# Layer 2's key, value and query products in a two-layer graph attention kernel: four-pass float32 against three float16 products

## The chip, the cores and the metric

The kernel runs on one core of a Trainium2 chip. The metric is the device time of one launch in microseconds (us). TensorE (PE) multiplies matrices, VectorE (DVE), ScalarE (ACT) and GpSimd (POOL) work element by element, SyncE (SP) issues nearly all DMAs.

## The reference

N = 3125 nodes with 128 features, and 103125 directed edges, self loops among them. Two TransformerConv layers run over the same edges, the first with 4 heads of 128 channels (512 features out, then relu), the second with 2 heads that are averaged. The result is added to x and each row is normalized.

```python
def transformer_conv(x, src, dst, Wq, bq, Wk, bk, Wv, bv, Ws, bs, H, C, concat):
    q = (x @ Wq + bq).reshape(n, H, C)      # k and v alike
    alpha = jnp.einsum('ehc,ehc->eh', q[dst], k[src]) / jnp.sqrt(jnp.float32(C))
    p = jnp.exp(alpha - amax[dst])          # softmax over the edges of a destination
    out = jax.ops.segment_sum(p[:, :, None] * v[src], dst, num_segments=n)
    out = out / denom[:, :, None]
    out = out.reshape(n, H * C) if concat else out.mean(axis=1)
    return out + x @ Ws + bs
h = jax.nn.relu(transformer_conv(x, ..., H1, C1, True))
out = transformer_conv(h, ..., H2, C2, False)
x = _layernorm(x + out, axis=-1)
```

## The kernel before

The graph is turned into a dense mask: a 3125 x 3125 table of the logarithm of how often each edge occurs, built in 87 batches (`mask_and_projections`) and kept in DRAM (`mask_scratch`). DVE compares edge ends with index rows ("hot" tiles), PE sums them, ACT takes the logarithm, SP stores it. Layer 1's K and V are computed between the batches. Attention is then dense: for each of 25 tiles of 125 destinations and each head there is one slot, numbered s, in which every engine does its share for slots s to s+3.

A slot of `attention` on PE has seven steps k. It holds the scores of 3125 sources in seven pieces, each three float16 products of a high and a low part (`scores`), 9 transposes of probabilities, 25 blocks of values (two float16 matmuls each, `product`), and at k=3 the query of slot s+3 (`query`). DVE adds the mask and takes the maximum (`masked_scores`), ACT does exponentials and high parts (`exponentials`, `part_hi`), POOL the low parts and the end of each row (`low_parts`, `finish`, `query_parts`), and SP's DMA transposes (`flip`) turn the first 16 blocks of probabilities. In layer 1's head 0, PE turns the finished rows of the tile before (`rows_transposed`, k=4) into PSUM bank `B_skip`, ACT applies the relu out of it, and PE then writes the tile's skip product into the same bank (`skip_product`, k=6), for which it waits for the relu (semaphore `s_r`). SP stores the relu's rows to `hT_scratch`.

Between the layers the hidden features hT (128 x 4 x 3125 float32, feature chunks k = 0 to 3 of 128) are loaded from `hT_scratch` into the tile `room`. `projections2` computes layer 2's K in 7 pieces of 512 nodes for 2 heads, and V in 25 blocks, each as four float32 matmuls accumulated in PSUM; ACT, POOL and DVE split the results. A float32 matmul is two records in the trace, and so x8 is one head's piece of K and x8 one block of V. Layer 2's queries are four float32 matmuls of 125 columns per slot, over 50 slots. `W` is the room of layer 2's weights, in the tile `spare`; POOL multiplies them in tiles 2 to 4 of layer 1 (`weights_scaled`).

The order of work on each engine is written out by hand in these functions, with semaphores between engines. Each block (mask, layer 1, projections, layer 2) ends when all engines have reached its end, SP with its last DMA issue too.

## Time and profile before

| | |
|---|---|
| median of 3 runs | 1863.93 us (1863.75 to 1864.02) |
| the profiled execution: time, span | 1863.01 us, 1861.2 us |
| PE, DVE, ACT, POOL busy | 95%, 81%, 67%, 61% |
| mean granted TensorE clock | 0.985 |
| mask and layer 1's K and V | 0 to about 220 us |
| layer 1's attention | about 225 to 1224 us |
| layer 2's K and V | 1226.8 to 1316 us |
| layer 2's attention | 1317.7 us to the end |

Busy time of PE is counted from the start to the modelled end of each matmul, and neighbours overlap, so a busy share near 100% says only that PE seldom stands idle. What a matmul costs in a dense stretch is the distance between the starts of neighbours.

### The profile page before, as it was taken

To read this page: it belongs to the slowest core of one execution; us is meant where nothing else is said; L and a number is where in the kernel's file an instruction comes from. 1 tells how busy PE (TensorE), PEld (TensorE's weight loads), DVE (VectorE), ACT (ScalarE), POOL (GpSimd) and SP (SyncE) were. 2 spreads that over 40 slices of the span, in tenths; PEclk is the share of its full clock that TensorE was granted. 3 is DMA by queue.
4 is the path that set the end of the run, shared out by engine and by line. 5 is a ranking of instruction groups with operands and counts; after the bars stand their busy time and mean duration, and the time that the engine had idled before them with its cause. 6 is when DMAs were issued, how large, how long until landed. Compare 5 with 4: busy or idle time off the path is not lost. (4 is left out here: it accounts for less than half of the span.)

```text
span 1861.2 us, 44238 instructions
## 1 busy us (share of the span) xinstructions
PE 1768.3 (95%) x14644; PEld 1328.6 (71%) x14644; DVE 1507.8 (81%) x4506; ACT 1255.4 (67%) x2090; POOL 1137.0 (61%) x1432
## 2 busy tenths in 40 slices
PE   3789799999999999999999999989899999999997
PEld 2556467777777777777777777756677787777876
DVE  7999889888888888888888788724688888988886
ACT  4579877777777677777777777721466667766675
POOL 4200067777776777777677776723477676766765
PEclk9899899999999999999999999999999999999999
DMA  6879868777888888888778887690488898888885
GB/s 164 221 210 264 233 116 151 156 148 151 159 157 156 154 150 157 159 154 154 152 156 153 159 159 151 117 255 4 88 173 169 182 174 179 174 179 180 181 176 109
DMA packets 753649, 301.72 MB, mean 162 GB/s; under 512 B 655853, under 2 KB 734065, under 8 KB 750171
## 3 DMA queue, kind: packets, MB, share of 16 engines
q1 hardware_dynamic: 752252, 296.96, 78.4%
q8 instruction: 122, 2.00, 0.5%
q0 software_dynamic: 640, 1.63, 0.3%
q14 instruction: 107, 0.87, 0.2%
q10 hardware_dynamic: 528, 0.26, 0.1%
HBM read 93.62 MB, written 47.83 MB: 76 GB/s over the span
## 5 line engine op out<-in xcount | busy, mean ns | idle before, releaser
L1383 POOL TENSOR_TENSOR prob_parts_l<-prob_l,prob_parts_l 125x512 f16<-125x512 f32 x600 | 721.2, 1233 | 13.5 <-ACT prob_parts_l L1470 13.5
L1461 ACT ACTIVATE prob_l<-prob_l,neg_max_l 125x1024 f32<-125x1024 f32 (+1 forms) x450 | 521.6, 1161 | 5.3 <-DVE neg_max_l L1553 5.3
L1729 PE MATMUL score_l<-room,QT_l 128*128 128x512 f16 (+2 forms) x2100 | 512.4, 353 | 1.4 <-DVE scale_rows L1701 1.2
L1476 ACT CAST probT_l<-transposed_l 128x375 f16<-128x375 f32 x450 | 213.5, 475 | 427.3 <-PE transposed_l L1753 427.3
L1768 PE MATMUL output_l<-V,prob_flipped_l 128*128 128x256 f16 x2400 | 459.6, 272 | 4.2 <-DMA prob_flipped_l<-prob_parts_l 4.1
L1770 PE MATMUL output_l<-V,prob_flipped_l 128*128 128x128 f16 x2400 | 427.5, 219 | 0.0
L1545 DVE CUSTOM_DVE_ANT_0 prob_l<-score_l,mask_even 125x512 f32<-125x512 f32 (+2 forms) x546 | 333.9, 615 | 113.7 <-PE score_l L1729 112.1
L1545 DVE CUSTOM_DVE_ANT_0 prob_l<-score_l,mask_odd 125x512 f32<-125x512 f32 (+2 forms) x504 | 308.9, 615 | 108.1 <-PE score_l L1729 106.9
L1470 ACT CAST prob_parts_l<-prob_l 125x1024 f16<-125x1024 f32 x300 | 309.5, 1033 | 0.1
L1768 PEld LDWEIGHTS output_l<-V,prob_flipped_l 128*128 128x128 f16 x2400 | 233.6, 97 | 56.5 <-issue 6.4
L1768 PE MATMUL output_l<-V,probT_l 128*128 128x256 f16 x1350 | 271.2, 273 | 2.8 <-DVE probT_l L1558 1.6
L1558 DVE TENSOR_TENSOR probT_l<-transposed_l,probT_l 128x375 f16<-128x375 f32 x450 | 244.9, 544 | 22.1 <-ACT probT_l L1476 14.0
L1729 PE MATMUL score_l<-KT,QT_l 128*128 128x512 f16 (+2 forms) x1050 | 255.1, 353 | 2.2 <-DVE piece_max_l L1545 2.2
L1770 PEld LDWEIGHTS output_l<-V,prob_flipped_l 128*128 128x128 f16 x2400 | 234.2, 98 | 28.5
L1729 PEld LDWEIGHTS score_l<-room,QT_l 128*128 128x128 f16 x2100 | 187.5, 98 | 91.5 <-issue 12.7
L1770 PE MATMUL output_l<-V,probT_l 128*128 128x128 f16 x1350 | 246.5, 219 | 0.0
L1371 POOL CAST QT_l<-q_now_l 128x125 f16<-128x125 f32 x150 | 43.8, 292 | 329.4 <-ACT q_now_l L1444 329.4
L1753 PE MATMUL transposed_l<-ident,prob_l 125*128 125x125 f32 (+1 forms) x1350 | 218.9, 270 | 5.9 <-ACT prob_l L1461 5.2
L1753 PEld LDWEIGHTS transposed_l<-ident,prob_l 125*128 125x128 f32 (+1 forms) x1350 | 171.7, 139 | 55.0 <-ACT prob_l L1461 3.8
L1768 PEld LDWEIGHTS output_l<-V,probT_l 128*128 128x128 f16 x1350 | 131.0, 97 | 67.3 <-DVE probT_l L1558 19.4
L1770 PEld LDWEIGHTS output_l<-V,probT_l 128*128 128x128 f16 x1350 | 131.8, 98 | 29.0
L1531 DVE SCALAR_TENSOR_TENSOR mask_even<-mask_even 125x512 f32<-125x512 f32 (+2 forms) x168 | 135.8, 808 | 0.0
(201 smaller groups left out, 2354.1 us busy)
## 6 DMA issues: line engine op xcount, KB each, us to landing
mask_scratch<-log SPq DMA_DIRECT2D x87, 420.0 KB
mask_even<-mask_scratch SPq DMA_DIRECT2D x25, 448.0 KB
mask_odd<-mask_scratch SPq DMA_DIRECT2D x24, 448.0 KB
mask_odd<-mask_scratch SPq DMA_DIRECT2D x12, 896.0 KB
mask_even<-mask_scratch SPq DMA_DIRECT2D x12, 896.0 KB
prob_flipped_l<-prob_parts_l SPq DMA_TRANSPOSE x600, 3.2
hT_scratch<-rowsT_l SPq DMA_DIRECT2D x24, 250.0 KB, 3.6
mask_odd<-mask_scratch SPq DMA_DIRECT2D x12, 471.2 KB
```

The source lines that it names most:

```text
L1371: pool.tensor_copy(QT[:, u, 0, 0:TP], q_now[:, u, :]).then_inc(s_qh, 1)
L1383: pool.tensor_tensor(parts[0:TP, 1, a:b], prob[:, h % 2, a:b], parts[0:TP, 0, a:b], ALU.subtract).then_inc(s_flo, 1)
L1461: act.activation(e, e, ACT.Exp, bias=neg_max[:, h % 2:h % 2 + 1], accum_out=total[:, h % 2, c:c + 1]).then_inc(s_exp, 1)
L1470: act.copy(parts[0:TP, 0, a:b], prob[:, h % 2, a:b]).then_inc(s_fhi, 1)
L1476: act.copy(probT[:, q, 0, 0:n, 0:TP], flipped_in_psum(h, q, n)).then_inc(s_hi, 1)
L1531: dve.scalar_tensor_tensor(piece, piece, STEEP, piece, ALU.mult, ALU.min).then_inc(s_cleared, 1)
L1545: dve.tensor_tensor_reduce(out=prob[:, h % 2, a:b], in0=score_bank(h, p)[0:TP, 0:b - a], in1=mask[parity][:, a:b], scale=1.0, scalar=-3.0e ...
L1558: dve.tensor_tensor(probT[:, q, 1, 0:n, 0:TP], flipped_in_psum(h, q, n), probT[:, q, 0, 0:n, 0:TP], ALU.subtract).then_inc(s_t, 1)
L1729: last = pe.matmul(score_bank(h, p)[:, 0:b - a], QT[:, h % 2, i, :], KT[:, h, j, a:b], start=n == 0, stop=n == len(products) - 1)
L1753: last = pe.transpose(flip_bank(h, q)[0:w, i * TP:(i + 1) * TP], prob[:, h % 2, b * C:b * C + w], ident[0:TP, 0:TP])
L1768: pe.matmul(O[:, 0:2 * C], hi, V[:, b, h, :, :].rearrange("p a c -> p (a c)"), start=start, stop=False, skip_group_check=True)
L1770: return pe.matmul(O[:, 0:C], lo, V[:, b, h, 0, :], start=False, stop=stop, skip_group_check=True)
```

## The change

Layer 2's K, V and queries become three float16 products each (high by high, high by low, low by high), twelve matmuls where there were four. For this hT and the weights are split into a float16 high and low part. The two parts of a feature lie next to each other, in the tile that is stored, in DRAM and in `room`, so that hT keeps its bytes and one part is read at a step of two float16. Before the split each hidden feature is brought into a fixed range: a power of two per feature is worked out from a bound (`h_row`, `h_up`) and multiplied into layer 1's skip weights, skip bias and `v_back`, and taken back out of layer 2's weights (`h_back`). The relu is now ACT's high part, and a new DVE instruction takes the low part (`rows_low`); `s_r`, for which PE's skip product and SP's store wait, is given by DVE. ACT's relu moves ahead of the third exponential. Layer 2's skip product stays float32: POOL joins the two parts of a tile's features first (`features`, into `h_now`). The weights are split in tiles 10 to 13 of layer 1, and lie first in `xT`'s room, since they are split in place.

```diff
+H_UP = 2.0 ** 3
+SPLIT_TILE = 10
+PRODUCTS = ((0, 0), (0, 1), (1, 0))
...
-    hT_dram = nc.dram_tensor("hT_scratch", (C, H1, N), F32, kind="Internal").ap()
+    hT_dram = nc.dram_tensor("hT_scratch", (C, H1, 2 * N), F16, kind="Internal").ap()
...
         room = sb("room", [C, H1 * N])
         spare = sb("spare", [C, 3 * H1 * H2 * C])
-        hT = room[:, :].rearrange("c (k n) -> c k n", k=H1)
+        hT = room[:, :].bitcast(F16).rearrange("c (k n a) -> c a k n", a=2, k=H1)
...
+                        dve.scalar_tensor_tensor(h_row, bank[7][:, :], TINY, abs_bs, ALU.max, ALU.add).then_inc(s_h_row, 1)
...
+                        dve.tensor_tensor(h_row, h_row, abs_rows[:, 2, :], ALU.add).then_inc(s_h_row, 1)
+                    if b == HIDDEN_AT + 1:
+
+                        dve.wait_ge(s_h_row, 2)
+                        dve.tensor_scalar(h_row.bitcast(I32), h_row.bitcast(I32), EXPONENT, None, ALU.bitwise_and).then_inc(s_h_row, 1)
+                        dve.wait_ge(s_h_row, 3)
+                        dve.tensor_scalar(h_up.bitcast(I32), h_row.bitcast(I32), -1, INVERSE_UP, ALU.mult, ALU.add).then_inc(s_h_row, 1)
...
+                        dve.tensor_scalar(second["h_back"][:, :], bank[LIST_BANK][:, 0:H1], 1.0 / H_UP, None, ALU.mult)
...
+                pool.wait_ge(s_h_row, 4)
+                for to, up in ((L["v_back"][:, :], h_up), (L["Ws"][:, 0, :], h_up), (L["bs"], h_up[0:TP, :])):
+                    pool.tensor_tensor(to, to, up, ALU.mult).then_inc(s_h_scaled, 1)
...
+                pool.wait_ge(s_late, 16)
+                pool.tensor_tensor(L["Ws"][:, :, :], L["Ws"][:, :, :], second["h_back"][:, :].unsqueeze(2).broadcast_to([C, H1, C]),
+                                   ALU.mult).then_inc(s_back, 1)
...
                         for k in range(H1):
-                            last = pe.matmul(bank[n % 2][:, 0:b - a], Wk_sb[:, k, h * C:(h + 1) * C],
-                                             hT[:, k, a:b], start=k == 0, stop=k == H1 - 1)
+                            for m, (i, j) in enumerate(PRODUCTS):
+                                last = pe.matmul(bank[n % 2][:, 0:b - a], Wk_sb[:, k, i, h * C:(h + 1) * C], hT[:, j, k, a:b],
+                                                 start=k == m == 0, stop=k == H1 - 1 and m == len(PRODUCTS) - 1)
...
                         for k in range(H1):
-                            last = pe.matmul(bank[2 + t % 2][0:r, 0:H2 * C], hT[:, k, t * C:t * C + r], Wv_sb[:, k, :],
-                                             start=k == 0, stop=k == H1 - 1)
+                            for m, (i, j) in enumerate(PRODUCTS):
+                                last = pe.matmul(bank[2 + t % 2][0:r, 0:H2 * C], hT[:, i, k, t * C:t * C + r], Wv_sb[:, k, j, :],
+                                                 start=k == m == 0, stop=k == H1 - 1 and m == len(PRODUCTS) - 1)
...
-                    sp.dma_start(hT_dram[:, :, bass.ds(t * TP, TP)], rowsT[:, :].rearrange("c (h n) -> c h n", h=H)
+                    sp.dma_start(hT_dram[:, :, bass.ds(2 * t * TP, 2 * TP)], rowsT_pairs[:, :, :].rearrange("c (h n) a -> c h (n a)", h=H)
...
+                def weights_back(n, i):
+
+                    w = second["W"][i]
+                    pool.wait_ge(s_scaled2, 2 * n + 1)
+                    pool.tensor_tensor(w, w, second["h_back"][:, :].unsqueeze(2).broadcast_to([C, H1, H2 * C]), ALU.mult
+                                       ).then_inc(s_scaled2, 1)
+
+                def features(t):
+
+                    wait(pool, s_sp, t)
+                    hi, lo = (featT[:, a, :, t * TP:(t + 1) * TP] for a in range(2))
+                    pool.tensor_tensor(h_now[:, :, :], hi, lo, ALU.add).then_inc(s_h_now, 1)
...
+                        if layer == 1 and h == 2 and 2 <= t <= 4:
+                            weights_back(t - 2, (0, 2, 1)[t - 2])
+                        if layer == 2 and h == 1 and exists(t + 1):
+                            features(t + 1)
...
-                        act.activation(rowsT[:, :], B_skip[:, 0:H * TP], ACT.Relu).then_inc(s_r, 1)
+                        act.activation(rowsT[:, 0, :], B_skip[:, 0:H * TP], ACT.Relu).then_inc(s_rhi, 1)
+
+                def weights_hi(n):
+
+                    act.wait_ge(s_scaled2, 6)
+                    if n == 0:
+                        act.wait_ge(s_sp, -(-H1 * H2 * C // TP))
+                    else:
+                        act.wait_ge(s_wlo, n)
+                    act.copy(w16_at[n][:, :, 0, :], second["W"][n]).then_inc(s_whi, 1)
...
-                            exponentials(s + 1, hn, 2)
                         if layer == 1 and h == 0 and not is_first(t):
                             rows_transposed(t - 1)
+                        if exists(tn):
+                            exponentials(s + 1, hn, 2)
+                        if layer == 1 and h == 2 and 0 <= t - SPLIT_TILE < 3:
+                            weights_hi(t - SPLIT_TILE)
...
+                def rows_low(t):
+
+                    dve.wait_ge(s_rhi, t + 1)
+                    if t == NT - 1:
+                        hi, lo = (hT[:, a, :, H_LATE:N] for a in range(2))
+                        dve.scalar_tensor_tensor(lo, B_skip[:, 0:H * TP].rearrange("c (k n) -> c k n", k=H), 0.0, hi,
+                                                 ALU.max, ALU.subtract).then_inc(s_r, 1)
+                    else:
+                        dve.scalar_tensor_tensor(rowsT[:, 1, :], B_skip[:, 0:H * TP], 0.0, rowsT[:, 0, :],
+                                                 ALU.max, ALU.subtract).then_inc(s_r, 1)
+
+                def weights_low(n):
+
+                    if n < 3:
+                        dve.wait_ge(s_whi, n + 1)
+                        dve.tensor_tensor(w16_at[n][:, :, 1, :], second["W"][n], w16_at[n][:, :, 0, :], ALU.subtract).then_inc(s_wlo, 1)
+                    else:
+                        dve.wait_ge(s_wlo, 3)
+                        dve.tensor_copy(second["W16"][0], first_w16).then_inc(s_w16, 1)
...
+                            if layer == 1 and h == 0 and k == 5 and not is_first(t):
+                                rows_low(t - 1)
+                            if layer == 1 and h == 3 and k == 3 and 0 <= t - SPLIT_TILE < 4:
+                                weights_low(t - SPLIT_TILE)
...
+                if layer == 1:
+                    rows_low(NT - 1)
...
-                    for k in range(KC):
-                        last = pe.matmul(B_q[:, 0:TP], Wq[:, k, h * C:(h + 1) * C], featT[:, k, bass.ds(t * TP, TP)],
-                                         start=k == 0, stop=k == KC - 1)
+                    if layer == 1:
+                        last = pe.matmul(B_q[:, 0:TP], Wq[:, 0, h * C:(h + 1) * C], featT[:, 0, t * TP:(t + 1) * TP],
+                                         start=True, stop=True)
+                    else:
+                        for k in range(KC):
+                            for m, (i, j) in enumerate(PRODUCTS):
+                                last = pe.matmul(B_q[:, 0:TP], Wq[:, k, i, h * C:(h + 1) * C], featT[:, j, k, t * TP:(t + 1) * TP],
+                                                 start=k == m == 0, stop=k == KC - 1 and m == len(PRODUCTS) - 1)
                     last.then_inc(s_qp, 1)
...
-                        last = pe.matmul(B_skip[0:TP, 0:W], featT[:, k, t * TP:(t + 1) * TP], Ws[:, k, :], start=k == 0, stop=k == KC - 1)
+                        pe.wait_ge(s_h_now, t + 1)
+                        for k in range(KC):
+                            last = pe.matmul(B_skip[0:TP, 0:W], h_now[:, k, :], Ws[:, k, :], start=k == 0, stop=k == KC - 1)
                     last.then_inc(s_sp, 1)
```

**Hand-over in layer 1.** The next rows are ACT's at the end of tile 1's head 0 in layer 1 (`prob_l` are probabilities, `prob_parts_l` their high parts, `rowsT_l` the relu's rows), before:

```order
L1444 ACTIVATE q_now_l<-query_l,bq_scaled_l 128x125
L1470 CAST prob_parts_l<-prob_l 125x1024
L1461 ACTIVATE prob_l,total_l<-prob_l,neg_max_l 125x1077
L1455 ACTIVATE rowsT_l<-skip_rows_l 128x500
L1476 CAST probT_l<-transposed_l 128x3x125 x3
```

and now:

```order
L1538 CAST prob_parts_l<-prob_l 125x1024
L1503 ACTIVATE q_now_l<-query_l,bq_scaled_l 128x125
L1538 CAST prob_parts_l<-prob_l 125x1024
L1514 ACTIVATE rowsT_l<-skip_rows_l 128x500
L1529 ACTIVATE prob_l,total_l<-prob_l,neg_max_l 125x1077
L1544 CAST probT_l<-transposed_l 128x3x125 x3
```

The relu changes places with the third exponential (125x1077). At the same place DVE has, at steps k=5 and 6 of head 0 (`ISA` rows are the masked scores and the reading of their maximum), before:

```order
L1576 TENSOR_SCALAR weight_l<-neg_max_l,inv_l 125x1
L1609 TENSOR_SCALAR scale_rows<-scale_rows 128x256
L1545 ISA prob_l,piece_max_l<-score_l,mask_odd 125x512
L1545 ISA piece_max_l 125x1
L1531 SCALAR_TENSOR_TENSOR mask_even<-mask_even 125x512
L1611 TENSOR_SCALAR scale_rows<-scale_rows 128x256
L1545 ISA prob_l,piece_max_l<-score_l,mask_odd 125x384
```

and now:

```order
L1680 TENSOR_SCALAR scale_rows<-scale_rows 128x256
L1616 ISA prob_l,piece_max_l<-score_l,mask_odd 125x512
L1616 ISA piece_max_l 125x1
L1705 SCALAR_TENSOR_TENSOR rowsT_l<-skip_rows_l,rowsT_l 128x500
L1602 SCALAR_TENSOR_TENSOR mask_even<-mask_even 125x512
L1682 TENSOR_SCALAR scale_rows<-scale_rows 128x256
L1616 ISA prob_l,piece_max_l<-score_l,mask_odd 125x384
```

The subtraction that makes the low part stands between the masked scores and the clearing of the next mask piece (`mask_even`). This recurs in each tile from 1 to 24.

**Layer 2's projections and queries on PE.** From the start of `projections2` (`room` is hT, `spare` the weights), before:

```order
L1168 MATMUL proj_bank<-room,spare 128x512 x4
L1158 MATMUL proj_bank<-ident,scale_rows 128x1 x4
L1168 MATMUL proj_bank<-room,spare 128x512 x4
L1178 MATMUL proj_bank<-spare,room 128x256 x16
L1168 MATMUL proj_bank<-room,spare 128x512 x8
L1178 MATMUL proj_bank<-spare,room 128x256 x16
```

and now:

```order
L1196 MATMUL proj_bank<-room,spare 128x512 x12
L1185 MATMUL proj_bank<-ident,scale_rows 128x1 x4
L1196 MATMUL proj_bank<-room,spare 128x512 x12
L1207 MATMUL proj_bank<-spare,room 128x256 x48
L1196 MATMUL proj_bank<-room,spare 128x512 x24
L1207 MATMUL proj_bank<-spare,room 128x256 x48
```

Each group is three times as long, and nothing moves. The query is alike: `query_l<-room,spare 128x125 x4` becomes x12 in every slot.

**Features on POOL.** The end of one of layer 2's tiles on POOL, from the head-0 slot's low parts, before:

```order
L1401 TENSOR_TENSOR rows_l<-summed_l,skip_l 125x128
L1371 CAST QT_l<-q_now_l 128x125
L1373 TENSOR_TENSOR QT_l<-q_now_l,QT_l 128x125
L1383 TENSOR_TENSOR prob_parts_l<-prob_l,prob_parts_l 125x512 x4
L1391 TENSOR_TENSOR summed_l<-summed_l,v_back 125x128
L1394 TENSOR_SCALAR summed_l<-summed_l,weight_l 125x128
L1404 TENSOR_TENSOR xres<-summed_l,rows_l 125x128
L1371 CAST QT_l<-q_now_l 128x125
L1373 TENSOR_TENSOR QT_l<-q_now_l,QT_l 128x125
L1383 TENSOR_TENSOR prob_parts_l<-prob_l,prob_parts_l 125x512 x4
```

and now:

```order
L1441 TENSOR_TENSOR rows_l<-summed_l,skip_l 125x128
L1411 CAST QT_l<-q_now_l 128x125
L1413 TENSOR_TENSOR QT_l<-q_now_l,QT_l 128x125
L1423 TENSOR_TENSOR prob_parts_l<-prob_l,prob_parts_l 125x512 x4
L1464 TENSOR_TENSOR h_now_l<-room 128x500
L1431 TENSOR_TENSOR summed_l<-summed_l,v_back 125x128
L1434 TENSOR_SCALAR summed_l<-summed_l,weight_l 125x128
L1444 TENSOR_TENSOR xres<-summed_l,rows_l 125x128
L1411 CAST QT_l<-q_now_l 128x125
L1413 TENSOR_TENSOR QT_l<-q_now_l,QT_l 128x125
L1423 TENSOR_TENSOR prob_parts_l<-prob_l,prob_parts_l 125x512 x4
```

One join of two parts (`h_now_l`) follows the low parts of every second slot, ahead of the end of the row.

## Rows read from the trace of the kernel before

**Rows 1.** Busy time by stretch: span, then PE, PEld, DVE, ACT, POOL, clock, DMA, GB/s.

```profile
140.00:170.00 30.00, 28.54 (x247) 19.33 (x245) 30.00 (x18) 29.62 (x44) 0.00 (x0) 1.00 0.98 268
240.00:1190.00 950.00, 944.87 (x8053) 708.95 (x8054) 788.40 (x2622) 692.42 (x1185) 686.59 (x870) 1.00 0.81 153
...
1340.00:1780.00 440.00, 437.79 (x3843) 347.57 (x3842) 376.64 (x1263) 295.32 (x504) 310.25 (x377) 1.00 0.87 176
```

**Rows 2.** Who waited in 1340 to 1780 us: total, times, longest.

```profile
POOL QT_l L1371 <- ACT q_now_l L1444: 92.0, 41, 3.3
DVE prob_l L1545 <- PE score_l L1729: 55.9, 68, 1.9
...
PE score_l L1729 <- DVE piece_max_l L1545: 2.2, 2, 2.0
```

**Rows 3.** PE in layer 2's projections: start, length, instruction.

```profile
1236.38 7.07 PE L1178 MATMUL proj_bank<-spare,room 128*128 128x256 f32 x32
1243.28 7.03 PE L1168 MATMUL proj_bank<-room,spare 128*128 128x512 f32 x16
1250.15 7.07 PE L1178 MATMUL proj_bank<-spare,room 128*128 128x256 f32 x32
```

**Rows 4.** PE at a query of layer 2, and what follows it.

```profile
1599.32 1.11 PE L1717 MATMUL query_l<-room,spare 128*128 128x125 f32 x8
1600.27 0.81 PE L1729 MATMUL score_l<-KT,QT_l 128*128 128x512 f16 x3
```

**Rows 5.** PE, eight value matmuls of layer 1, each with its weight load.

```profile
564.05 0.27 PE L1768 MATMUL output_l<-V,prob_flipped_l 128*128 128x256 f16 x1
564.16 0.22 PE L1770 MATMUL output_l<-V,prob_flipped_l 128*128 128x128 f16 x1
...
564.71 0.65 PE L1729 MATMUL score_l<-room,QT_l 128*128 128x384 f16 x3
```

**Rows 6.** PE, a batch of the mask: twelve 160-column matmuls, each with a weight load.

```profile
151.71 0.99 PE L954 MATMUL mask_banks<-hot 128*128 128x160 bf16 x12 [0.19 <-DVE hot L782]
152.53 1.04 PE L917 MATMUL mask_banks<-xT,Wk_sb 128*128 128x500 f32 x2
```

**Rows 7.** Layer 1, head 0 of one tile: ACT, DVE and PE from step k=5.

```profile
564.23 1.20 ACT L1461 ACTIVATE prob_l<-prob_l,neg_max_l 125x1077 f32<-125x1077 f32 x1
...
565.05 0.97 DVE L1531 SCALAR_TENSOR_TENSOR mask_odd<-mask_odd 125x512 f32<-125x512 f32 x1
...
565.41 0.57 ACT L1455 ACTIVATE rowsT_l<-skip_rows_l 128x500 f32<-128x500 f32 x1
...
566.03 0.29 PEld L1739 LDWEIGHTS skip_rows_l<-Ws_sb,xT 128*125 128x125 f32 x2 [0.24 <-ACT rowsT_l L1455]
...
567.49 0.48 PE L1753 MATMUL transposed_l<-ident,prob_l 125*128 125x125 f32 x3
```

**Rows 8.** The tile skip_rows_l: DVE's add from PSUM, and the waits on the relu.

```profile
L1681 DVE TENSOR_TENSOR skip_l<-skip_rows_l,bias_room x25: 677/681/692, 252.9 to 1196.9; 125x512 f32<-125x512 f32 x25
...
  ACT rowsT_l L1455: 5.5, 23
```

**Rows 9.** Groups by line: a small DVE step of the mask, POOL's low parts.

```profile
L254 DVE TENSOR_SCALAR room<-v_back 128x512 int32<-128x512 int32 x1 | 0.4, 427 | 0.0
...
L1383 POOL TENSOR_TENSOR prob_parts_l<-prob_l,prob_parts_l 125x512 f16<-125x512 f32 x600 | 721.2, 1233 | 13.5 <-ACT prob_parts_l L1470 13.5
```

**Rows 10.** DVE in the mask stage, while POOL works and after it.

```profile
55.41 3.20 DVE L782 TENSOR_TENSOR hot<-row_iota,rel 128x2880 bf16<-128x2880 f16 x1
...
64.38 1.66 DVE L782 TENSOR_TENSOR hot<-row_iota,rel 128x2880 bf16<-128x2880 f16 x1
```

**Rows 11.** The end of layer 1: SP's issue of loads, the last relu, the first product.

```profile
1220.83 5.31 SPq L1360 DMA_DIRECT2D room<-hT_scratch  x2
...
1224.08 0.59 ACT L1452 ACTIVATE room<-skip_rows_l 128x500 f32<-128x500 f32 x1 [8.18 <-PE skip_rows_l L1745]
...
1226.84 5.08 PE L1168 MATMUL proj_bank<-room,spare 128*128 128x512 f32 x8 [2.79 <-PEq L1294]
```

More of the change, by code:

```diff
@@ L99 @@
 INVERSE = 254 << 23
+INVERSE_UP = (254 + 3) << 23
 EPS_DENOM = 1e-16
@@ L333, in mask_and_projections @@
         bv_sb, abs_ws = (k_room[:, 2 * N + i * H1 * C:2 * N + (i + 1) * H1 * C] for i in range(2))
-        abs_bs, h_row = (k_room[0:1, 2 * N + i * H1 * C:2 * N + (i + 1) * H1 * C] for i in range(2, 4))
+        abs_bs, h_row = (k_room[:, 2 * N + i * H1 * C:2 * N + (i + 1) * H1 * C] for i in range(2, 4))
+        h_up = abs_bs
         minus = sb("minus_ident", [C, C], F16)
@@ L1430, in _ @@
                 low_parts(0, 0)
+                if layer == 2:
+                    features(0)
                 over_tiles(tile)
@@ L1726, in scores @@
                     wait(pe, s_masked, NP * s + p + 1 - score_bank_back(h, p))
[L1727 to L1728 removed]
+                    for n, (i, j) in enumerate(PRODUCTS):
                         last = pe.matmul(score_bank(h, p)[:, 0:b - a], QT[:, h % 2, i, :], KT[:, h, j, a:b],
[L1730 removed]
+                                         start=n == 0, stop=n == len(PRODUCTS) - 1)
                     last.then_inc(s_score, 1)
@@ L1735, in skip_product @@
                         wait(pe, s_r, t)
+                        last = pe.matmul(B_skip[0:TP, 0:W], featT[:, 0, t * TP:(t + 1) * TP], Ws[:, 0, :], start=True, stop=True)
                     else:
                         wait(pe, s_skip, t)
-                    for k in range(KC):
-                        last = pe.matmul(B_skip[0:TP, 0:W], featT[:, k, t * TP:(t + 1) * TP], Ws[:, k, :], start=k == 0, stop=k == KC - 1)
+                        pe.wait_ge(s_h_now, t + 1)
+                        for k in range(KC):
+                            last = pe.matmul(B_skip[0:TP, 0:W], h_now[:, k, :], Ws[:, k, :], start=k == 0, stop=k == KC - 1)
                     last.then_inc(s_sp, 1)
```

53 lines of the change are left out of this document (32 added, 21 removed).

## Prediction

> **What bounds the kernel now.** I read the busy time by stretch first [rows 1]. In layer 1 (240 to 1190 us) and layer 2 (1340 to 1780 us) PE is busy 99% of the time at a granted clock of 1.00, DVE 83% and 86%. Busy is not bound, so the waits come next [rows 2]: in 440 us of layer 2 PE waited 2.2 us for DVE's maxima, DVE 55.9 us for PE's scores and POOL 92.0 us for the query that PE starts. PE sets the pace there; a microsecond taken from its queue is a microsecond of the span, as long as DVE keeps its 55.9 us in hand. In the projections PE's groups follow each other without a gap: K's two heads of a piece (x16) start 6.87 us before the next group, four blocks of V (x32) 6.90 us [rows 3]. The mask stage is different: in 140 to 170 us DVE is busy for all of 30.00 us [rows 1], so what is added to DVE there lengthens the stage.
>
> **K and V.** A head's piece of K takes 6.87 / 2 = 3.44 us, a block of V 6.90 / 4 = 1.73 us. The price of a float16 product I take from eight value matmuls, four of 256 and four of 128 columns, each with its own weight load: 564.05 to 564.71, 0.66 us for 1536 columns [rows 5], 0.43 ns a column, 0.22 us for 512 columns, 0.11 us for 256. Twelve make 2.64 us and 1.32 us. K gives back 12 x 0.80 = 9.6 us, and the last piece of 53 columns some 0.5 us (estimated as 2 x 12 products at 0.055 us, the price of 128 columns, against the same four passes); V 25 x 0.41 = 10.2 us. Together 20.3 us. The split after them keeps up: DVE has per block of V two steps of 256 columns (some 0.35 us each, half of the 0.68 us for 512 [rows 8]) and a clearing of up to 0.97 us [rows 7], 1.6 us against 1.32 us on PE. In four blocks it falls 1.1 us behind, less than the one block that the second bank holds, and K's two heads (5.3 us) let it catch up. I charge 0.5 us for this and for the weight splits below.
>
> **Queries.** A query takes 1600.27 - 1599.32 = 0.95 us [rows 4]. Twelve products of 125 columns cost 12 x 0.43 x 125 = 0.65 us by the column, 12 x 0.055 = 0.66 us by the same rows. All 50 queries lie on PE's path: 14.5 us. Here nothing of before shows 125-column products one behind the other, each with a weight load. The nearest row is the mask's batch, twelve products of 160 columns in 152.53 - 151.71 = 0.82 us, 0.068 us each [rows 6], which is the columns' price again (160 x 0.43 = 0.069), so no floor shows at 0.068. Bounds: 0.82 us a query (saves 6.5 us), and 0.65 us (15 us). I take 0.66, since within the value matmuls a 128-column product with its load does fit into 0.055 us: the pair of 256 and 128 takes 0.165, of which the 256 columns need 0.11.
>
> The Trainium skill says otherwise ("TensorE: Matmul & The Clock Gate", Back-to-back issue gap): pairs of weight load and matmul are said to sustain about 81 ns per matmul at 128 columns. By it a query would be 0.97 us and the queries would give back nothing; the value matmuls and the mask's 0.068 us speak against it.
>
> **The step of two float16.** hT is read as moving operand (K, queries) and loaded as weights (V) at a step of two elements, 4 bytes. No row shows this. Rows at both ends: contiguous float16 moves 2 bytes per 0.43 ns. Float32 with its four passes moves 4 bytes per column and pass in two records, 0.43 us per record of 512 columns [rows 3], that is 4.8 bytes per ns, just as contiguous float16 has 4.7. If bytes spanned were the limit, a stepped product would cost 0.43 us per 512 columns, twice my price. I take the column's price, as columns per pass explain all rows too (512 columns in two passes at 2.4 GHz), and keep the other as a rival.
>
> The Trainium skill ("SBUF — State Buffer", Door 1: The DMA port swizzle) has accesses to one 16-byte line at full bandwidth if at least two hit it, a free step of up to 8 bf16; a step of two hits four times and would be free. No run yet shows it.
>
> **Hand-over in layer 1.** PE's skip product waits for the relu 23 times, 5.5 us in all [rows 8], 0.24 us each. In the tile shown ACT starts the third exponential at 564.23 and the relu at 565.41, and PE goes on at 566.03 [rows 7]. Now the relu comes first and ends at about 564.23 + 0.57 = 564.80, and DVE, which is free at 565.05, subtracts: 0.68 us for 500 columns out of PSUM, from the add of the same bank [rows 8], to 565.73, before PE gets there at about 565.8. The wait goes: -4.5 us (bounds: -5.5, and +3 if DVE is 0.1 us later than the relu was). The exponential ends 0.57 us later, at about 566.1; its reader on PE starts at 567.49 [rows 7], so 1.4 us cover it. Behind the subtraction on DVE stand a clearing of the mask and the next masked scores, which have the slack that DVE has each slot. If that cover were gone, 24 x 0.68 = 16 us would stand there. SP's store of the rows waits for DVE instead of ACT and gets its rows earlier.
>
> **The mask stage.** DVE gets two small steps of 512 columns, 0.43 us each [rows 9], and one of 4 columns: +1.0 us. POOL gets three multiplications of 512 columns, about 1.2 us each [rows 9], 3.7 us. DVE's comparison of 2880 columns takes 3.20 us while POOL works and 1.66 us when it doesn't [rows 10]: 1.54 us lost in 3.20. By that 3.7 us of POOL cost DVE 1.5 us (0 to 1.8). Sum +2.5 us (1 to 3).
>
> **What is hidden.** POOL's join of features, 25 of about 1.2 us [rows 9], stands behind the low parts, and POOL waits 92.0 us in 42 slots for queries [rows 2], 2.2 us a slot. Without this cover it would be 30 us. The row's end is 1.2 us later and has its next reader a slot on. POOL's three multiplications of weights (1024 columns, some 2.5 us each by twice the price of 512) in layer 1 meet the same wait. ACT's three casts and DVE's four steps for the weights, about 1 us each, take ACT's and DVE's idle time, in four tiles; bounded by 4 us. At the end of layer 1 the low part of the last rows comes 0.7 us after the relu (1224.67), at 1225.4; SP issues loads until 1220.83 + 5.31 = 1226.14 and PE starts at 1226.84 [rows 11], so SP still ends the block. DMAs carry the same bytes in the same runs. The multiplication of Ws on POOL in `projections2` waits for a load; the first cast behind it may be 1 us late, while PE has one bank more to fill. PE's start at a lower clock (5.08 us for a piece of 3.44 [rows 11]) stays as it is.
>
> **Sum.** -20.3 - 14.5 - 4.5 + 2.5 + 0.5 = -36.3 us. The profiled execution took 1863.0 us, 0.9 us less than the median: 1826.7 us, and 1827.6 us against the median.
>
> **Rivals.**
> - The step costs (moving operand at half rate). K: 12 x (12 x 0.43 - 3.44) = +20.6 us; a query 12 x 0.43 x 125 x 2 = 1.29 us, +17 us; V and the rest as above: -10.2 - 4.5 + 3.0. Sum +26 us: 1890 us, slower. It decides from a price of about 1.5 columns per column on. For it: nothing excludes it; against it: passes explain the rows as well. 9%.
> - Products of 125 columns with a load have a floor at 0.068 us or above (0.08 us: the rule above). The queries give 6.5 us or nothing: 1836 to 1842 us. The rows speak against it. 10%.
> - Something in layer 1 takes the place of the removed wait: PE waits for DVE's subtraction, or DVE, pushed back 0.68 us, hands PE its maxima later. +0.2 us in each of 24 tiles instead of -0.2: 1837 us; that DVE is idle for 17% of layer 1 [rows 1] speaks against it. 9%.
> - Layer 2 does not stay with PE: after 0.29 us less a slot DVE's idle time of 1.3 us a slot shrinks to 1.0, and POOL is 1.2 us busier in every second slot. A third of the queries' gain lost, with some of the joins: 1835 us. 10%.
> - The forecast, all terms about as above: 62%, own range 1821 to 1834 us.
>
> **Numbers.** 1827.6 us. The forecast and its three rivals on the same side reach from 1821 to 1842 us; with the bounds of the small terms I give 1820 to 1846 us, which leaves the stepped case and some mishap out. A difference of 0.2%, 3.7 us, is about what a measurement of this kernel can tell from none. Faster 0.89, same 0.02, slower 0.09.
>
> **What would show it.** Right: K's group of a piece about 5.3 us instead of 6.87, V's of four blocks 5.3 instead of 6.90, a query 0.66 us from its start to the next instruction, no wait for `rowsT_l` before the skip product, layer 1's attention begun 2 to 3 us later, DVE's idle time in layer 2 lower and PE's waits still a few us. Wrong: matmuls of `room` whose starts lie 0.43 us apart for 512 columns (the step), 0.08 us for 125 (the load), PE waiting for `rowsT_l` of DVE or `piece_max_l` in layer 1, or for `h_now_l` in layer 2.

## Result and the profile after

| | before | after |
|---|---|---|
| median, 4 runs each | 1863.97 us (1863.75 to 1864.87) | 1842.86 us (1840.68 to 1843.64) |
| ratio, 95% interval | | 0.9884 (0.9867 to 0.9901) |
| profiled span | 1861.2 us | 1841.3 us |
| PE, DVE, ACT, POOL busy | 95%, 81%, 67%, 61% | 95%, 85%, 69%, 64% |

The changed kernel is 21 us faster, where 36 us were forecast: the direction and the range held, the size did not. Two places answer well to the rows of before. In layer 2's projections PE's groups are (start, length, instruction; they answer to [rows 3]):

```profile
1239.06 5.62 PE L1196 MATMUL proj_bank<-room,spare 128*128 128x512 f16 x24
1244.52 5.40 PE L1207 MATMUL proj_bank<-spare,room 128*128 128x256 f16 x48
1249.76 5.62 PE L1196 MATMUL proj_bank<-room,spare 128*128 128x512 f16 x24
```

K's group now starts 5.46 us before the next one, not 6.87, and V's 5.24 us, not 6.90. And a query of layer 2, with what follows it (answers to [rows 4]), takes 0.70 us, not 0.95:

```profile
1646.95 0.86 PE L1819 MATMUL query_l<-room,spare 128*128 128x125 f16 x12
1647.65 0.81 PE L1830 MATMUL score_l<-KT,QT_l 128*128 128x512 f16 x3
```

The places where the time went are found by PE's first query of each stage. These rows are the first query of layer 1, the first of layer 2, and one of head 0 in tile 16 and in tile 24 of layer 2, after:

```profile
228.91 0.54 PE L1814 MATMUL query_l<-xT,Wq_sb 128*128 128x125 f32 x1 [6.27 <-PEq L501]
...
1297.85 0.89 PE L1819 MATMUL query_l<-room,spare 128*128 128x125 f16 x7 [2.82 <-PEq L1083]
...
1626.31 0.86 PE L1819 MATMUL query_l<-room,spare 128*128 128x125 f16 x12
...
1791.56 0.62 PE L1819 MATMUL query_l<-room,spare 128*128 128x125 f16 x8
```

| place | before | after | moved by | forecast |
|---|---|---|---|---|
| first query of layer 1 | 225.07 | 228.91 | +3.8 | +2.5 |
| a query of layer 1's last tile | 1179.49 | 1178.18 | -5.2 | -4.5 |
| first query of layer 2 | 1317.72 | 1297.85 | -18.6 | -20.3 + 0.5 |
| end of the span | 1861.2 | 1841.3 | 0.0 | -14.5 |

("moved by" counts from the row above.) So what is missing is missing in layer 2's attention. Outside it, the mask stage lost 1.3 us more than forecast and the projections gave 1.2 us less, and the hand-over in layer 1 gave 0.7 us more. Each query of layer 2 is 0.25 us shorter, fifty of them, and the attention is as long as it was (543.5 us both; 541.2 us in e11, a second trace of the changed kernel). The waits of 440 us of it, 1320 to 1760 us (answers to [rows 2]):

```profile
POOL QT_l L1411 <- ACT q_now_l L1503: 77.7, 42, 5.6
DVE prob_l L1616 <- PE score_l L1830: 40.0, 48, 1.5
PEld output_l L1871 <- DVE probT_l L1629: 16.3, 40, 1.0
...
PE score_l L1830 <- DVE piece_max_l L1616: 3.0, 2, 2.7
```

DVE's wait for scores fell from 55.9 to 40.0 us. The third row is new among the first: PE's weight loads for the value matmuls wait 40 times for DVE's low part of `probT`, which stands in the queue just behind the query. PE got there earlier and DVE did not. The same wait in 440 us of before, and of the runs e2 and e1 below, whose queries are longer and shorter than the changed kernel's:

```profile
PEld output_l L1768 <- DVE probT_l L1558: 1.7, 6, 0.3
PEld output_l L1874 <- DVE probT_l L1629: 1.7, 5, 0.5
PEld output_l L1870 <- DVE probT_l L1629: 23.3, 47, 1.8
```

It grows as the query shrinks. A weight load runs ahead of the matmuls, so only a part of these waits holds up the products themselves.

A table of how long a tile (two heads) of layer 2 takes helps below. Each number is the distance of two first queries of tiles, divided by the tiles between them (eight or nine, tiles 15 or 16 to 24); after, (1791.56 - 1626.31) / 8.

| kernel | PE in a query | a tile |
|---|---|---|
| before | 0.95 us | 20.95 us |
| after | 0.70 us | 20.66 us |
| e1, 4 products | 0.23 us | 20.16 us |
| e2, 17 products | 0.99 us | 21.03 us |
| e3, features joined once | 0.70 us | 20.51 us |
| e7, skip product in float16 | 0.70 us | 20.31 us |

### The profile page after: what moved, and what is told of

The parts are those of the page before. It is cut to its first block and busy times, and to the rows that moved or that the text cites. A ratio compares the mean times of both kernels' runs of the same rounds, so it can differ in the third digit from the quotient of the medians.

```text
span 1841.3 us, 45045 instructions
## 1 busy us (share of the span) xinstructions
PE 1742.8 (95%) x15000; PEld 1301.7 (71%) x15000; DVE 1561.1 (85%) x4538; ACT 1262.7 (69%) x2093; POOL 1175.7 (64%) x1464
## 5 line engine op out<-in xcount | busy, mean ns | idle before, releaser
L1602 DVE SCALAR_TENSOR_TENSOR mask_even<-mask_even 125x512 f32<-125x512 f32 (+2 forms) x168 | 151.1, 899 | 0.0
```

The source lines that it names most:

```text
L1602: dve.scalar_tensor_tensor(piece, piece, STEEP, piece, ALU.mult, ALU.min).then_inc(s_cleared, 1)
```

## Experiments

Ratios are to the kernel before, timed beside each. The theories: (A) VectorE takes over the pace of layer 2's slots, (B) PE keeps it and the gain is lost elsewhere, (C) GpSimd's new work slows VectorE.

**How much a query's time is worth.** e1_short_query puts one product in place of three (it leaves out the crossed ones), e2_long_query puts five more in front of them, as here:

```diff
+                        for r in range(5):
+                            pe.matmul(B_q[:, 0:TP], Wq[:, r % KC, 0, h * C:(h + 1) * C], featT[:, 0, r % KC, t * TP:(t + 1) * TP],
+                                      start=True, stop=True)
```

> Layer 2's queries sum the high-by-high products alone: 4 products instead of 12, so a query is about 0.46 us shorter on TensorE (0.69 to 0.23 at 0.0575 us a product); the crossed products of the queries are left out. Theory A: in layer 2 VectorE's chain sets the slot, and what TensorE saves it spends waiting for VectorE's low part of probT; then 50 x 0.46 = 23 us off TensorE give little, 1837 to 1843. Theory B: TensorE sets the slot and the missing gain is lost elsewhere (the joined features on GpSimd, the clock at the layer's start); then nearly all comes through, about 1820.

> Layer 2's queries get five more products ahead of their sum (17 instead of 12), so a query takes about 0.69 + 5 x 0.0575 = 0.98 us, as long as it took in float32 (0.95). Theory A (VectorE sets the slot of layer 2): 50 x 0.29 = 14 us more on TensorE show as 0 to 5 us, 1843 to 1848. Theory B (TensorE sets it): about 1857.

e1: 1827.57 us, ratio 0.9803 (0.9789 to 0.9816), 14 to 15 us less than the changed kernel (against its second and first series, e11) for 23 us of PE. e2: 1850.29 us, 0.9924 (0.9911 to 0.9938), 7 to 9 us more for 14.5. Neither theory alone: in a tile e1 takes 0.92 us from PE and gets 0.50 us, e2 adds 0.59 us and pays 0.37. With the joins on GpSimd in place, about half to two thirds of PE's time reaches the slot, on both sides of the changed kernel. The tile of e2 is 0.08 us longer than that of the kernel before (21.03 against 20.95 us), which is what its two queries take more: behind a query of that length the joins cost nothing.

**The joined features.** e3_features_once leaves 24 of 25 additions out; each tile's skip product reads the first tile's features.

```diff
-                        if layer == 2 and h == 1 and exists(t + 1):
-                            features(t + 1)
...
-                        pe.wait_ge(s_h_now, t + 1)
+                        pe.wait_ge(s_h_now, 1)
```

> GpSimd joins the two parts of layer 2's features for the first tile only, and every tile's skip product reads that one; 24 additions of 1.035 us go from GpSimd, and the skip rows of tiles 1 to 24 are those of tile 0. Theory C: these additions slow VectorE beside them (mask clears and low parts); 25 us of such overlap at the ratio of row 10 would give 5 to 10 us back, 1833 to 1838. Theory A or B without it: 1841 to 1844.

1837.33 us, 0.9857 (0.9842 to 0.9873): 4 to 5.5 us less, near the small end of theory C. The work that I had put down as hidden costs what lies beside it on DVE. Groups by form in layer 2, DVE's clearing of 384 columns of the mask, after:

```profile
L1602 DVE SCALAR_TENSOR_TENSOR mask_odd<-mask_odd 125x384 f32<-125x384 f32 x24 | 17.1, 713 | 0.0
```

and in e3:

```profile
L1600 DVE SCALAR_TENSOR_TENSOR mask_odd<-mask_odd 125x384 f32<-125x384 f32 x24 | 13.2, 550 | 0.0
```

The chain in one tile of after, POOL's join first, then DVE's clearing and its low part of `probT`, then PE's scores and the first value matmul behind the query (which starts at 1636.13):

```profile
1634.97 1.02 POOL L1464 TENSOR_TENSOR h_now_l<-room 128x500 f32<-128x500 f16 x1
...
1635.48 0.92 DVE L1602 SCALAR_TENSOR_TENSOR mask_even<-mask_even 125x384 f32<-125x384 f32 x1
...
1636.99 0.54 DVE L1629 TENSOR_TENSOR probT_l<-transposed_l,probT_l 128x375 f16<-128x375 f32 x1
...
1636.83 0.81 PE L1830 MATMUL score_l<-KT,QT_l 128*128 128x512 f16 x3
1637.59 0.28 PE L1871 MATMUL output_l<-V,probT_l 128*128 128x256 f16 x1
```

and at the same place in e3, where the query starts at 1630.06:

```profile
1629.41 0.55 DVE L1600 SCALAR_TENSOR_TENSOR mask_even<-mask_even 125x384 f32<-125x384 f32 x1
...
1630.55 0.54 DVE L1627 TENSOR_TENSOR probT_l<-transposed_l,probT_l 128x375 f16<-128x375 f32 x1
...
1630.77 0.81 PE L1828 MATMUL score_l<-KT,QT_l 128*128 128x512 f16 x3
1631.41 0.27 PE L1869 MATMUL output_l<-V,probT_l 128*128 128x256 f16 x1
```

The clearing starts inside the join, which ends at 1635.99, and takes 0.92 instead of 0.55 us. The low part begins 0.86 us behind the start of the query instead of 0.49, and PE's value matmul 0.76 us behind its scores instead of 0.64. So 0.12 us of what the shorter query gave is lost at the very next wait; behind the longer queries of before and e2 this distance is 0.65 us in every tile. In 440 us of e3 the wait for `probT` is 7.7 us in place of 16.3. A tile takes 20.51 us without the joins, 0.15 less; the rest is in tile 13 (e10 below), where the slots last 12.0 and 12.7 us in e3 against 12.0 and 15.0 after.

**The step of two.** e4_parts_apart stores and keeps high and low parts apart, so that nothing is read or written at a step; each row has one feature of padding.

```diff
-        hT = room[:, :].bitcast(F16).rearrange("c (k n a) -> c a k n", a=2, k=H1)
+        hT = room[:, :].bitcast(F16).rearrange("c (a k n) -> c a k n", a=2, k=H1)
...
-            rowsT_pairs = sb("rowsT", [C, H * TP, 2], F16)
-            rowsT = rowsT_pairs[:, :, :].rearrange("c n a -> c a n")
+            rowsT = sb("rowsT", [C, 2, H * TP], F16)
```

> High and low parts of the hidden features stand apart in the tile, in DRAM and on chip (each row padded by one feature), so every product, the relu and the low part read or write without a step; two stores and two loads instead of one. If the step of two is free on TensorE, as the 0.0575 us a product suggests, and the longer relu (0.73 us against 0.57) is hidden: 1841 to 1845. If the step costs TensorE a tenth of the 650 products of projections and queries or the relu's length is on layer 1's path: 3 to 8 us less, 1835 to 1840.

1847.12 us, 0.9902 (0.9887 to 0.9917): 4 to 6 us slower than the changed kernel, outside both expected ranges. For the step the group is what counts. V's products in the projections load hT's parts as weights, after:

```profile
L1207 PE MATMUL proj_bank<-spare,room 128*128 128x256 f16 (+1 forms) x300 | 34.2, 273 | 0.0
```

and with the parts apart:

```profile
L1207 PE MATMUL proj_bank<-spare,room 128*128 128x256 f16 (+1 forms) x300 | 34.2, 273 | 0.0
```

Not a nanosecond between them. K's products read hT as moving operand. With the parts apart a group of 24 starts 5.18 us before the next one, against 5.46 us at the step of two (1239.06 to 1244.52 above):

```profile
1245.60 5.34 PE L1196 MATMUL proj_bank<-room,spare 128*128 128x512 f16 x24
1250.78 5.40 PE L1207 MATMUL proj_bank<-spare,room 128*128 128x256 f16 x48
```

That is 0.216 against 0.228 us a product, and it is so in all full groups. The products of a query, too, start 55 instead of 58 ns apart. So the step costs a moving operand 5% and a weight load nothing. ACT's relu takes 0.73 us at a step and 0.59 us without. What made the kernel slower are the pieces' loads, twice as many: PE's sequencer held the first product of the projections for 9.1 us against 2.9. K's shorter groups gave some 1.5 us of it back; the shorter queries did not shorten the tiles (20.78 us).

**The hand-over in layer 1.** e5_relu_last puts ACT's relu back behind the third exponential.

```diff
-                        if layer == 1 and h == 0 and not is_first(t):
-                            rows_transposed(t - 1)
                         if exists(tn):
                             exponentials(s + 1, hn, 2)
+                        if layer == 1 and h == 0 and not is_first(t):
+                            rows_transposed(t - 1)
```

> ScalarE's relu goes back behind the third exponential of its step in layer 1; its float16 output and VectorE's low part stay. If the earlier relu is what freed TensorE in layer 1, the wait for it comes back and with it the gain of 4.8 us read between the first query of layer 1 and the end of that layer: 1846 to 1849. If the gain came from something else (the shape of the layer's last steps): 1842 to 1844.

1867.70 us, 1.0014 (1.0005 to 1.0023): 25 us more than the changed kernel, where I expected 5. The waits on the tile `rowsT_l` in e5 (us, times), of which there are none after:

```profile
who waited for it (us, times):
  PEld skip_rows_l L1837: 26.5, 24
  DVE rowsT_l L1705: 23.9, 24
```

One tile of it:

```profile
575.70 0.71 ACT L1514 ACTIVATE rowsT_l<-skip_rows_l 128x500 f16<-128x500 f32 x1
...
576.45 0.71 DVE L1705 SCALAR_TENSOR_TENSOR rowsT_l<-skip_rows_l,rowsT_l 128x500 f16<-128x500 f32 x1 [1.03 <-ACT rowsT_l L1514]
...
577.22 1.12 PE L1837 MATMUL skip_rows_l<-Ws_sb,xT 128*125 128x512 f32 x2 [0.91 <-DVE rowsT_l L1705]
```

The low part is a second link behind the relu. With the old order the wait is the old 0.24 us [rows 8], plus the relu's longer float16 form (0.15), plus DVE's step (0.7): 1.1 us in each of 24 tiles, and layer 1 is 1.0 us longer for each than after. I had expected the relu's old wait alone and left out that DVE's step now stands behind the relu.

**The mask stage.** e6_narrow_scaling shrinks GpSimd's three multiplications to 8 columns and leaves the others unscaled, e9_scale_on_vector gives them to VectorE.

```diff
-                for to, up in ((L["v_back"][:, :], h_up), (L["Ws"][:, 0, :], h_up), (L["bs"], h_up[0:TP, :])):
+                for to, up in ((L["v_back"][:, 0:8], h_up[:, 0:8]), (L["Ws"][:, 0, 0:8], h_up[:, 0:8]), (L["bs"][:, 0:8], h_up[0:TP, 0:8])):
                     pool.tensor_tensor(to, to, up, ALU.mult).then_inc(s_h_scaled, 1)
```

```diff
-                pool.wait_ge(s_h_row, 4)
-                for to, up in ((L["v_back"][:, :], h_up), (L["Ws"][:, 0, :], h_up), (L["bs"], h_up[0:TP, :])):
-                    pool.tensor_tensor(to, to, up, ALU.mult).then_inc(s_h_scaled, 1)
...
+                        dve.wait_ge(s_h_row, 4)
+                        for to, up in ((L["v_back"][:, :], h_up), (L["Ws"][:, 0, :], h_up), (L["bs"], h_up[0:TP, :])):
+                            dve.tensor_tensor(to, to, up, ALU.mult).then_inc(s_h_scaled, 1)
```

> GpSimd's three multiplications of the hidden rows' scale into value scales, skip weights and skip bias cover 8 columns instead of 512 in the mask stage (the other columns stay unscaled). If these 6.5 us of GpSimd are what makes the mask stage 3.8 us longer rather than 2.5, through VectorE's hot products beside them: first attention query 1 to 2.5 us earlier, 1840.5 to 1842. If it is VectorE's own three wide steps on the hidden row: no change, 1842 to 1844.

> The three multiplications by the hidden rows' scale in the mask stage go from GpSimd (3.0, 2.4 and 1.1 us) to VectorE, behind the row's scale. The run with 8 columns on GpSimd was 4.7 us faster than the changed kernel. If GpSimd's work beside VectorE's hot products is the cost (one hot product of 1.7 us takes 3.2 beside it), VectorE pays instead 3 x 0.6 = 1.8 us of its own: 1839 to 1841. If it is the transfer of the work and not its place: 1842.5 to 1845.

e6: 1838.16 us, 0.9865 (0.9850 to 0.9880), 3 to 5 us less than the changed kernel and more than was expected, its first query at 224.71, 4.2 us earlier than after and 0.4 earlier than before. So the multiplications were the whole loss. (The place moves by itself: in ten other runs with the changed kernel's mask stage the first query starts between 228.2 and 231.7 us, never near 224.7.) They are, after:

```profile
76.66 3.00 POOL L711 TENSOR_TENSOR Ws_sb<-Ws_sb,room 128x512 f32<-128x512 f32 x1
79.62 1.13 POOL L711 TENSOR_TENSOR bias_room<-bias_room,room 125x512 f32<-125x512 f32 x1
```

and DVE beside them, after:

```profile
75.66 3.05 DVE L799 TENSOR_TENSOR hot<-col_iota,rel 128x3840 bf16<-128x3840 f16 x1
78.63 1.18 DVE L777 TENSOR_SCALAR V<-V 128x256 f32<-128x256 int32 x1
79.84 1.06 DVE L778 TENSOR_SCALAR V<-V 128x256 f32<-128x256 f32 x1
...
91.48 0.69 DVE L788 TENSOR_SCALAR rel<-mask_banks 128x512 f16<-128x512 f32 x1 [1.91 <-ACT rel L557]
```

The same four in e6:

```profile
75.59 2.15 DVE L799 TENSOR_TENSOR hot<-col_iota,rel 128x3840 bf16<-128x3840 f16 x1
77.67 0.28 DVE L777 TENSOR_SCALAR V<-V 128x256 f32<-128x256 int32 x1
77.98 0.29 DVE L778 TENSOR_SCALAR V<-V 128x256 f32<-128x256 f32 x1
...
87.20 0.69 DVE L788 TENSOR_SCALAR rel<-mask_banks 128x512 f16<-128x512 f32 x1 [0.26 <-ACT rel L557]
```

DVE lost 0.90 + 0.90 + 0.77 = 2.6 us directly and 1.65 us more in its next wait for ACT, 4.2 in sum. A step of 0.28 us took 1.18 and ended at 79.81, just after POOL's multiplication (79.66). e9: 1843.30 us, 0.9887 (0.9871 to 0.9904), first query at 228.96: nothing won, as the second of its two expectations had it. DVE's three steps start 0.6 us apart, 1.8 us in all, but DVE then waits 1.5 us for ACT at 104.84. Of e9's 4.25 us against e6, 1.8 are DVE's own work; why the rest comes back in that wait for ACT I did not settle. Only leaving the work out was shown to win; taking it off GpSimd was not.

**The skip product in float16.** e7_skip_f16 drops the joined features and splits layer 2's skip weights ahead of the layer.

```diff
+                pool.tensor_copy(L["Ws16"][:, :, 0, :], L["Ws"][:, :, :]).then_inc(s_back, 1)
...
-                        pe.wait_ge(s_h_now, t + 1)
                         for k in range(KC):
-                            last = pe.matmul(B_skip[0:TP, 0:W], h_now[:, k, :], Ws[:, k, :], start=k == 0, stop=k == KC - 1)
+                            for m, (i, j) in enumerate(PRODUCTS):
+                                last = pe.matmul(B_skip[0:TP, 0:W], featT[:, i, k, t * TP:(t + 1) * TP], L["Ws16"][:, k, j, :],
+                                                 start=k == m == 0, stop=k == KC - 1 and m == len(PRODUCTS) - 1)
```

> Layer 2's skip product too is three float16 products from the parts of the features, its weights split once ahead of the layer; the joined features (25 x 1.035 us of GpSimd) are gone. The run that joined once stood at 1837.3, so 5.5 us come from GpSimd's additions being gone; the product itself goes from 4 float32 to 12 float16 products, 1.1 to about 0.7 us, 25 times 0.4 = 10 us of TensorE, of which half came through for the queries: 5 more. Together 1831 to 1834. If the skip product's end is hidden (nothing but GpSimd's part comes): 1836 to 1838.

1831.91 us, 0.9831 (0.9817 to 0.9844): 9.5 to 11 us less than the changed kernel, within the expected range. A tile goes from 20.66 to 20.31 us: 0.15 for the joins, 0.20 for the skip product. What that gave to PE is the distance to the next scores, after:

```profile
1641.21 1.09 PE L1842 MATMUL skip_rows_l<-Ws_sb,h_now_l 128*125 128x128 f32 x8
1642.14 0.65 PE L1830 MATMUL score_l<-KT,QT_l 128*128 128x384 f16 x3
```

and in e7:

```profile
1635.09 0.89 PE L1834 MATMUL skip_rows_l<-Ws_f,room 128*125 128x128 f16 x12
1635.81 0.65 PE L1822 MATMUL score_l<-KT,QT_l 128*128 128x384 f16 x3
```

It is 0.93 us and then 0.72, so 0.21 us of PE gave 0.20 us a tile: all of it came through. The expected range was hit by luck. It took 0.4 us of PE, from the busy length of 1.1 us, and let half of it through.

**The start of layer 2.** e8_busy_gap fills PE's pause ahead of the layer.

```diff
+                wait(pe, s_k, 2 * n)
+                for i in range(10):
+                    pe.matmul(bank[0][:, 0:512], Wk_sb[:, 0, 0, 0:C], hT[:, 0, 0, 0:512], start=True, stop=True)
```

> TensorE does ten more products of 512 columns (about 2.2 us) in the 2.8 us in which it waited between layer 2's projections and its first query. The clock granted at 1300 to 1305 us was 0.55; the first three slots of the layer took 2.2 us longer than before. If the pause is what lowered the clock: 1 to 2.2 us less, 1840.5 to 1842. If the clock falls for another reason, or if the filled stretch delays the layer: 1842.5 to 1845.

Windows of 5 us (span, PE, PEld, DVE, ACT, POOL busy, granted clock, DMA share, GB/s), after:

```profile
1295.00:1300.00 5.00, 1.72 (x16) 1.46 (x16) 3.86 (x10) 0.77 (x3) 1.05 (x3) 0.77 0.22 56
1300.00:1305.00 5.00, 5.00 (x23) 2.50 (x21) 2.72 (x8) 0.36 (x1) 1.26 (x4) 0.55 0.18 53
```

and in e8:

```profile
1295.00:1300.00 5.00, 4.55 (x41) 2.75 (x38) 4.08 (x12) 1.30 (x6) 2.49 (x5) 1.00 0.00 0
1300.00:1305.00 5.00, 4.36 (x34) 2.19 (x31) 4.57 (x11) 0.73 (x2) 1.44 (x4) 1.00 0.44 113
```

After a pause of 2.8 us the clock stood near the lower of its levels (0.5 of full, 1.2 GHz); without the pause it stays at full speed, and the third query starts 6.6 us after the first instead of 9.0. Before the change the pause was 1.8 us and the clock stayed at 1.00. In time the filled pause can't be told: 1841.20 us, 0.9872 (0.9857 to 0.9888). In e11's trace, the changed kernel again, the third query comes 7.5 us after the first; 1 to 2.4 us of the layer's start go with the clock, by the execution.

**Normed rows.** e10_norms_spread moves twelve normed rows from tile 13 to tiles 13 to 18, and their two stores to tiles 17 and 20 (not shown).

```diff
-NORMS_AT = {(13, h, k): (6 * h + k - 1,) for h in range(2) for k in range(1, 7)}
+NORMS_AT = {(13 + i, 1, k): (2 * i + (k == 5),) for i in range(6) for k in (2, 5)}
```

> The first twelve normed rows of layer 2 go from tile 13 (one in each step of its slots) to two a tile in tiles 13 to 18, their stores to tiles 17 and 20. The slots at that place took 12.0 and 15.0 us where 10.8 and 9.8 are the rule, 6.4 us too long (2.6 before the change), and 12.0 and 12.7 where the features were joined once. If VectorE is full there and the burst pushes it over: 3 to 6 us less, 1837 to 1840. If the burst is late for another reason (the square roots' table on ScalarE, the transposed parts' transfers): 1841 to 1844.

1837.60 us, 0.9859 (0.9843 to 0.9875), 4 to 5 us less; the slots of tile 13 take 10.9 and 9.9 us where they took 12.0 and 15.0. VectorE was full there (busy 27.3 of 28 us from 1588 to 1616 us after). Before, the same rows cost 11.0 and 12.6 us, 2.6 us over a normal tile; after, 6.3 us over it.

**The changed kernel again.**

> The changed kernel once more, unaltered, on the chip and beside the runs of the others: 1841 to 1844.5, so that differences of 2 us between runs can be weighed.

1841.37 us, 0.9888 (0.9871 to 0.9904). Two series of it differ by 1.5 us, so differences of 2 us between kernels prove nothing here, and those above are given against both.

**Together.** e12_together has the edits of e7, e8 and e10.

> Three of the edits that helped, in one kernel: layer 2's skip product in float16 (11 us less than the changed kernel alone), ten products in TensorE's pause ahead of layer 2 (1 us), and the first twelve normed rows spread over six tiles (4 us). If they add up: about 16 us less than 1841 to 1843, so 1825 to 1828. If the normed rows and the joined features had paid the same slots of tile 13 and 14 (12.0 and 14.3 us without the features, so that most of it is left for the norms): the sum holds within 1 us; if VectorE takes back half of what is freed: 1829 to 1833.

1827.24 us, 0.9805 (0.9791 to 0.9818): 14 to 16 us less than the changed kernel and 37 less than before. They nearly add up. With the joins gone, in its 440 us of layer 2 the wait on `probT` is less than half of that after:

```profile
PEld output_l L1867 <- DVE probT_l L1624: 6.9, 21, 0.6
```

## Why the prediction was right in direction and short in size

- **K and V** (-20.3, measured -18.6): right. V's blocks cost 5.24 us for the 5.3 worked out, K's pieces 5.46 for 5.3, and 5.18 where nothing is read at a step (e4); six pieces of K at 0.18 us more are 1.1 us, and PE's pause before the first query grew from 1.8 to 2.8 us, since the casts and low parts of the last block are now waited for by an earlier PE.
- **The price of a product** (0.055 us with its weight load): right without the step (55 ns in e4), 0.70 / 12 = 0.058 us with it. Fifty queries gave PE 12.5 us and not 14.5. The Trainium skill's 81 ns per matmul at 128 columns ("TensorE: Matmul & The Clock Gate", Back-to-back issue gap) would make this query 0.97 us; the trace has 0.70. The rival of a floor falls.
- **The step of two** was put at nothing. It is free where hT is loaded as weights and costs 5% where it is the moving operand: 6 x 0.28 us in K and some 50 x 0.04 us in the queries, 3.7 us of PE. The rival of 1890 us, which needs a product at twice the price, falls. By "SBUF — State Buffer" of the Trainium skill (Door 1: The DMA port swizzle) such a step would be free; the trace agrees for the weight loads (109 ns a product both ways), and for the moving operand it differs by those 5% (228 against 216 ns).
- **The hand-over** (-4.5, measured -5.2): right, and more fragile than the text had it. The relu's place is not worth 5 us but 25, since with the old order the change loses 24 x 1.0 us (e5); the rival "takes its place" named this wait with +0.2 us a tile, a fifth of its price.
- **The mask stage** (+2.5, measured +3.8): the term was made of 1.0 us of DVE's own steps, which don't show (e6 begins its attention no later than before), and 1.5 us for POOL, which cost 4.2. I had spread the measured loss of [rows 10] over 3.7 us of POOL (1.8 us by that ratio, entered as 1.5); POOL's three took 6.5 us beside DVE's comparisons (in e6, with 8 columns, the first two still took 1.5 and 2.1 us), and DVE then missed its place with ACT.
- **The queries** (-14.5, measured 0.0 over layer 2's attention) is the step that failed. "PE sets the pace there; a microsecond taken from its queue is a microsecond of the span" was read from the waits of before, where PE waited 2.2 us. It holds where DVE is not waited for: with the joins left out the first 0.25 us of a query gives 0.44 us a tile for 0.50 (e3), and the skip product 0.20 for 0.21 (e7). With the joins it is 0.29 for 0.50, and 0.50 for the next 0.92 (e1). The condition "as long as DVE keeps its 55.9 us in hand" was read as a sum over all steps. At the one wait behind the query, for `probT`, there was nothing left once the query was shorter and the join delayed DVE: that wait is 1.7 us before and 16.3 after. The account of layer 2: 23 tiles shorter by 0.29 us, -6.7; tile 13 worse by 3.7 us (6.3 against 2.6 over a normal tile); the first two queries' stretch longer by 2.2 us with the clock (9.0 against 6.8); one wait of 1.0 us for a transposed part. Sum +0.2, measured 0.0 in this execution and -2.2 in e11's (1.5 of it in the stretch with the clock).
- **"What is hidden"** was wrong for POOL's joins: 4 to 5.5 us by e3. I had asked whether POOL has time for them, and not what they do to DVE, though [rows 10] showed it and the mask stage's term used it. It is the same mistake in both places. The rival "layer 2 does not stay with PE" named both mechanisms with 7 us. They cost up to 9.5 of the 14.5 missing (5.8 in the tiles, where PE was given 12.5 and 6.7 came through, and 3.7 in tile 13); the rest is the price of the step (2.0), the clock (2.2) and one transposed part (1.0).

The Trainium skill has the mechanism ("SBUF — State Buffer", SBUF: two separate sides): VectorE, in the steps that use it, and GpSimd share a pair of ports as an exclusive lock, held for a whole instruction, and the other one blocks. The trace agrees where a DVE step of 0.28 us ends 0.15 us after POOL's multiplication, and where the masked scores, which read PSUM, keep their 0.68 us all through. What it doesn't tell is why GpSimd's 8 columns took 1.5 and 2.1 us in e6; no run here separates that.

## What to carry to other kernels

An engine that waits for nobody sets the pace only until it is shortened. How much of a saving comes through is decided at the next wait behind the shortened work, not by the total that the other engine has in hand: before counting a saving in full, look at what stands right behind the shortened work and at who delivers it, and try the slope with a few dummy or omitted instructions. Work that is put on an idle GpSimd is not free while VectorE works from on-chip memory beside it; count the overlap as VectorE's time. Price a change on an engine that runs dense by the distance to the next instruction, and not by its busy length. When a value gets a second step (high, then low part), both links stand in the hand-over, and the order of the first decides over both.

## What the runs showed of the hardware

- Twelve float16 products of 125 columns, each with its own weight load, take 0.70 us when the moving operand is read at a step of two elements, 0.66 us when the moving operand is contiguous. Reading a float16 moving operand at a step of two elements costs 5% (0.228 against 0.216 us for 512 columns); loading weights at that step costs nothing (109 ns a product of 256 columns both ways). ScalarE's relu from PSUM takes 0.73 us when it writes float16 at a step of two and 0.59 without the step.
- A VectorE step of 0.28 us took 1.18 us beside a GpSimd multiplication, and GpSimd's multiplications of 512 columns took 2.4 and 3.0 us beside VectorE's comparisons and 1.1 us when VectorE was the one that was held up.
- After a pause of 2.8 us in TensorE's work the granted clock of the next 5 us was 0.55 (0.75 in a second trace of the same kernel, after the same pause); with the pause filled it was 1.00, and after a pause of 1.8 us in the kernel before it was 1.00 too.
